# Two tanh to a step, and who copies the turned exponentials, in the interleaved attentions of an audio tower

## The reference, cut to what matters

```python
# third: one head, every query with every key through 16 tanh units
hid = tanh(hq[:, :, None, :] + hk[:, None, :, :] + b1)
attn = softmax(Q @ K.T / sqrt(128) + hid @ W2 + b2);  out = attn @ V
# fourth: 8 heads, causal
dot = where(causal, (x @ Wq.T / s) @ (x @ Wk.T / s).T, -inf)   # s = 128 ** 0.25
out = (softmax(dot) @ (x @ Wv.T)) @ Wo.T, summed over heads
```

## Time and profile before

| | us |
|---|---|
| median of 3 runs | 4598.27 (4597.84 to 4599.58) |
| the profiled execution, its own time | 4594.98 |
| its span, first to last instruction | 4593.1 |
| mean granted TensorE clock | 0.946 |
| busy, share of the span | PE 91%, DVE 61%, ACT 63%, POOL 15% |
| `tail()`, from about 3040 to the end | about 1550 |
| three passes of last with additive attention, each | about 240 |
| of each, the stretch that has tanh in it | 150 to 153 |
| last attention alone (sequence 3) | about 144 |

### The profile page before, as it was taken

One profiled execution on the slowest core, in us unless ns is written; L12 is line 12 of the kernel. 1 busy time (PEld: TensorE's weight loads), 2 busy tenths in 40 slices (PEclk: granted clock), 3 DMA queues, 4 the chain that ended last, 5 costly groups with the idle time before them and its releaser, 6 DMA issues.

```text
span 4593.1 us, 67780 instructions
## 1 busy us (share of the span) xinstructions
PE 4165.6 (91%) x25119; PEld 2334.1 (51%) x25119; DVE 2788.3 (61%) x6459; ACT 2872.6 (63%) x6125; POOL 692.7 (15%) x466
## 2 busy tenths in 40 slices
PE   6788779999999999999999999968888888997988
PEld 4454434444444444444444444434556655665666
DVE  5655567777777777777777777622343344245254
ACT  1222247877787877778777777765664474474533
POOL 0000112222222222222222222100000000000000
PEclk9877779999999999999999999979999999999999
DMA  2000034333342424242433424000100000100000
GB/s 108 1 28 0 21 45 53 46 46 55 41 69 37 57 43 53 50 53 44 52 50 53 57 36 59 24 31 24 36 1 19 26 1 10 31 1 1 28 4 4
DMA packets 94423, 160.53 MB, mean 35 GB/s; under 512 B 18272, under 2 KB 75024, under 8 KB 93712
## 3 DMA queue, kind: packets, MB, share of 16 engines
q1 hardware_dynamic: 94096, 156.20, 20.4%
HBM read 74.04 MB, written 7.82 MB: 18 GB/s over the span
## 4 chain that ended last, share of the span: by engine, by line
PE 74%; DVE 9%; issue 6%; ACT 6%; DVEq 2%; PEld 1%; POOL 1%; DMA 1%; PEldq 0%; POOLq 0%; SPq 0%; ACTq 0%
PE ps L1151 12%; PE ps L1187 12%; PE ps L1161 10%; PE ps L1507 9%; PE ps L1221 4%; PE ps L1230 4%; PE ps L1142 2%; PE ps L1038 2%; PE ps L1639 2%; PE ps L1250 2%; PE ps L1439 2%; DVE peaks L2225 2%; PE ps L1601 1%; PE ps L1577 1%; PE ps L1023 1%
## 5 line engine op out<-in xcount | busy, mean ns | idle before, releaser
L2225 DVE TENSOR_REDUCE peaks<-ps 128x1 f32<-128x748 f32 (+1 forms) x1536 | 1408.4, 933 | 481.8 <-PE ps L1161 459.6
L1796 ACT ACTIVATE masked<-ps 128x384 f32<-128x384 f32 (+3 forms) x1536 | 683.1, 486 | 197.2 <-PE ps L1151 185.0
L1796 ACT ACTIVATE probs<-ps 128x384 f32<-128x384 f32 (+1 forms) x1536 | 662.3, 484 | 74.1 <-PE ps L1151 73.6
L912 POOL TENSOR_TENSOR rstd<-var,minus_half 128x6 f32<-128x6 f32 x104 | 138.3, 1329 | 2875.2 <-DVE var L2458 1484.5
L1151 PE MATMUL ps<-shared 98*128 98x384 bf16 (+3 forms) x1536 | 447.3, 327 | 4.4 <-ACT probs L1796 1.7
L1151 PE MATMUL ps<-q_stack,k_stack 98*128 98x384 bf16 (+3 forms) x1536 | 449.9, 328 | 0.9
L1161 PE MATMUL ps<-k_stack,q_stack 96*128 96x374 bf16 (+1 forms) x1536 | 380.7, 329 | 37.0 <-DMA k_stack<-parts 21.5
L1161 PE MATMUL ps<-shared 96*128 96x374 bf16 (+1 forms) x1536 | 372.1, 323 | 8.7 <-DVE peaks L2225 8.0
L1151 PEld LDWEIGHTS ps<-shared 98*128 98x128 bf16 (+1 forms) x1536 | 147.9, 103 | 336.6 <-ACT masked L1796 125.9
L1151 PEld LDWEIGHTS ps<-q_stack,k_stack 98*128 98x128 bf16 (+1 forms) x1536 | 149.7, 103 | 328.4 <-ACT masked L1796 121.2
L1161 PEld LDWEIGHTS ps<-k_stack,q_stack 96*128 96x128 bf16 (+1 forms) x1536 | 154.6, 105 | 159.4 <-DVE peaks L2225 44.3
(11 more groups left out here) (571 smaller groups left out, 7684.6 us busy)
## 6 DMA issues: line engine op xcount, KB each, us to landing
shared<-parts SPq DMA_DIRECT2D x192, 187.0 KB, 9.2
wr<-in_l SPq DMA_DIRECT2D x32, 580.5 KB, 3.5
q_stack<-parts SPq DMA_DIRECT2D x96, 187.0 KB, 7.8
k_stack<-parts SPq DMA_DIRECT2D x96, 187.0 KB, 10.3
wts<-in_l SPq DMA_DIRECT2D x32, 514.5 KB, 3.6
wrow<-in_l_rows SPq DMA_DIRECT2D x32, 320.0 KB, 4.1
wq<-in_l SPq DMA_DIRECT2D x32, 192.0 KB, 3.3
const<-in_const SPq DMA_DIRECT2D x1, 4202.5 KB, 12.9
```

The lines of the kernel that those rows point to most:

```text
L912: pool.tensor_tensor(lane.rstd, lane.var, minus_half[:, :], ALU.pow).then_inc(S["rstd_ready"], 1)
L1796: act.activation(probs_ring(u)[0:m, 0:hi - lo], src[0:m, 0:hi - lo], ACT.Exp, scale=float(HD) ** -0.5).then_inc(S["ring_done"], 1)
L2225: v.tensor_reduce(peaks[0:m, g, j, head:head + 1], src[0:m, :, 0:T // 2], XY, ALU.max)\
```

## The change

Two edits. Each step `add` of four tanh (cost 3.95) becomes a step `add` (2.1) and a step `more` (1.85), two tanh each on ACT (the wait for a free buffer in the first, `hidden_ready` in the second, the exponentials of L1944 at the start of the second). The other engines do in `add` what they did and nothing in `more`. And ACT copies half 0 of the turned exponentials as well as half 1; DVE's L2591 goes.

```diff
-        steps += [(("add", u, q), 3.95) for u in range(NT) for q in range(4)]
+        steps += [step for u in range(NT) for q in range(4)
+                  for step in ((("add", u, q), 2.1), (("more", u, q), 1.85))]
...
-                def add(lane, k, u, q):
-                    if u == 0 and q == 0:
+                def add(lane, k, u, q, more=False):
+                    if u == 0 and q == 0 and not more:
                         act.drain()
                         used[0] = n.now("hidden_used")
+                        n.take(f"spread0_{k}", 2 * NT)
                         n.take("hidden_used", 4 * NT)
...
-                    if quad and s >= TANH_SLOTS:
+                    if quad and s >= TANH_SLOTS and not more:
                         act.wait_ge(S["hidden_used"], used[0] + s - TANH_SLOTS + 1)
-                    for i, (g, _) in enumerate(quad):
+                    first, end = (2, len(quad)) if more else (0, 2)
+                    for i, (g, _) in list(enumerate(quad))[first:end]:
                         if q == 1 and u and i == 2:
                             exponentials(lane, k)
...
-                    if quad:
+                    if quad and more:
                         last.then_inc(S["hidden_ready"], 1)
-                    elif q == 1:
+                    elif q == 1 and not quad:
                         exponentials(lane, k)
...
                 def last(lane, k, i):          # ACT
                     what, e, u = last_entry(i - SPREAD_LAG)
+                    if what == "score":
+                        tiles = min(3, u + 1)
+                        act.wait_ge(S[f"spread0_{k}"], n.take(f"spread0_{k}"))
+                        act.activation(flat(last_probsT(lane, i - SPREAD_LAG)[:, 0:tiles, :]),
+                                       ps[:, SPREAD_BANK, 0:tiles * P], ACT.Copy).then_inc(S[f"taken0_{k}"], 1)
...
                 def last(lane, k, i):          # DVE
-                    what, e, u = last_entry(i - SPREAD_LAG)
-                    if what == "score":
-                        tiles = min(3, u + 1)
-                        v.wait_ge(S[f"spread0_{k}"], n.take(f"spread0_{k}"))
-                        v.tensor_copy(flat(last_probsT(lane, i - SPREAD_LAG)[:, 0:tiles, :]),
-                                      ps[:, SPREAD_BANK, 0:tiles * P]).then_inc(S[f"taken0_{k}"], 1)
```

More of the change, by code:

```diff
@@ L1945, in exponentials @@
                                    accum_out=lane.total[:, 0:1]).then_inc(S[f"probs_ready_{k}"], 1)
-                def add(lane, k, u, q):
-                    if u == 0 and q == 0:
+                def add(lane, k, u, q, more=False):
+                    if u == 0 and q == 0 and not more:
                         act.drain()
                         used[0] = n.now("hidden_used")
+                        n.take(f"spread0_{k}", 2 * NT)
                         n.take("hidden_used", 4 * NT)
-                    if q == 0 and u < 2:
+                    if q == 0 and u < 2 and not more:
                         act.wait_ge(S["query_part_ready"], n.take("query_part_ready"))
                     quad, s = ADDITIVE[u][q] if u < NT else (), 4 * u + q
-                    if quad and s >= TANH_SLOTS:
+                    if quad and s >= TANH_SLOTS and not more:
                         act.wait_ge(S["hidden_used"], used[0] + s - TANH_SLOTS + 1)
-                    for i, (g, _) in enumerate(quad):
+                    first, end = (2, len(quad)) if more else (0, 2)
+                    for i, (g, _) in list(enumerate(quad))[first:end]:
                         if q == 1 and u and i == 2:
@@ L2036, in tail @@
                         mixed(lane, k, *at)
-                    elif what == "add":
-                        add(lane, k, *at)
+                    elif what in ("add", "more"):
+                        add(lane, k, *at, what == "more")
                     elif what == "pool":
@@ L2613, in last @@
                         v.drain()
+                        n.take(f"spread0_{k}", len(LAST_UNIT))
                 def logits(lane, k):
```

## The result

The changed kernel takes 4702.23 us (median of 4 runs, 4701.43 to 4708.41) against 4598.06 of the kernel before in the same rounds: a ratio of 1.0229, 95% interval 1.0211 to 1.0247. It is 104 us slower. The forecast was 4650 (+52) and the range ended at 4686: sign and place were right, the size was about half, and the time lies outside the range.

What follows compares the result with a forecast made beforehand. PE was taken to carry the time, with each in-order handover between ACT and PE adding to it. 3 x (19 - 4) + 9 = +54 us gave 4652, written as 4650 (chance 0.62), range 4608 to 4686.

Steps and rivals of the forecast that it cites:

- Last attention alone, +9: Last attention of sequence 3: half 0 copies queued on ACT cost 1.1 us a head, 8 heads; bounds 5 and 12.
- The 0.83 at u = 5: Last attention alone: ACT's copy stands behind the exponential of u = 4, so PE goes on 0.83 us late.
- u = 4: Last attention alone: ACT copies the queries first, so PE turns half 1 of this entry 0.25 us late.
- the small entries: Last attention alone: covered by 0.5 us or more of other PE work; up to 0.5 each where uncovered.
- End of a pass, -4: After the last tanh: DVE sheds copies, PE no longer waits for them behind pooling and gating; -1 to -6 us.
- Tanh stretch, +19: Per pass: PE waits for ACT's late copies and tanh; +16.9 us in 116 walked, some 2 elsewhere; bounds 8 and 26.
- the walk: Tanh stretch, L29 to L37 stepped through in the new order with old durations: five PE waits, +6.7 us; three neighbours likewise.
- the sparser rest, 36 us, adds some 2: The 36 us of a tanh stretch outside the four heads from L13 to L45: some 2 us more a pass.
- The finer steps pay: Rival: halved tanh blocks halve PE's idle time in the tanh stretch, -8 a pass; total -30, 4568 us; chance 0.10.
- Only the copy counts: Rival: tanh stretch only +6 a pass, end -4, last attention alone +9; total +15, 4613 us; chance 0.15.
- The clock falls too: Third rival: five more half-rate spells a pass after PE waits, 3 x 8.5 = +25 on top, 4677 us; chance 0.13.
- The upper bound: Tanh stretch: 26 us a pass, the worst segment's rate throughout, 6.7 / 26.2 of 152, less a third for the sparse end.

Runs made afterwards that it cites:

- the kernel with the wide copies only: Kernel before, steps of four tanh kept, with ACT copying half 0 only for entries u = 5, 3, 4: 4660.97 us, ratio 1.0134.
- the mildest form: Kernel before with only ACT's tanh split into steps of two; PE and DVE keep their old order, DVE its copy: 4604.17 us, ratio 1.0011.
- the fillers: Against the kernel with ACT copying half 0 for u = 5, 3, 4: 8 unused matmuls before PE's u = 5 wait, last attention alone: 4655.83 us.

## Why the prediction was right in direction and short in size

- **Where the kernel is bound: right.** PE carried the time, ACT had 36 us to spare and has 58 now; the kernel still lost, because what counts is when ACT reaches a copy. The five waits for copies and four for L1944 were read from PEld, the weight loads; the matmuls themselves waited three times for each, 5.3 and 3.5 us.
- **Last attention alone, +9: right in size** (+11.5), in part by luck. The seven later heads take 1.16 us more each (18.00 for 16.84) against 1.1 predicted; the first takes the other 3.4, with a half-rate spell in it.
- **How that +11.5 came about is only in part as walked.** The 0.83 at u = 5 came out in the kernel with the wide copies only. In a later head of the changed kernel PE's half 1 of u = 5 is 0.33 late: its wait is 0.75 for 0.61, and a new one of 0.48 for the copy of u = 2 stands where PE waited 0.51 for its next score slot before. u = 4 adds 0.27, as predicted (0.25), and the copy of u = 1, ahead of its weigh, some 0.5. The prediction had the small entries down as covered and took nothing for them into the sum. Five other kernels that leave this stretch as it was have 144.8 there, not 143.4, with 3.5 to 4.5 us more at half rate at its start, so one trace doesn't fix the length within a microsecond.
- **End of a pass, -4: right size (-3.5), wrong reason.** Fewer waits give 0.8; the rest is work that moved out and clock, and the ends are as short with the steps alone. The copy on ACT only there (-10 us, of which the ends show 6) confirms the direction, not the size.
- **Tanh stretch, +19: the step that failed**, in two terms. First, the walk itself held: five waits within 0.4 us each, four heads 18.8 for 16.9. But "the sparser rest, 36 us, adds some 2" was put down without a walk, and it measured 5.5: the first and the sixth head have 2.1 and 3.8 us more idle time, like the others. Rest and walk together are 5 of the 16 us that were missed. Second, the walk's durations were all those at full rate, and the clock stood beside the sum as a rival with 0.13. It measured 18 us more at half rate a pass, 9 us of lost work; the third rival (five more spells, +8.5 a pass) was right in mechanism and in the number of spells. Together 19 + 5 + 9 = 33, and 2 us are matmuls from the end.
- **The rivals.** "The finer steps pay" is refuted three times: with the old copies (+43, and +5 even in the mildest form), with ACT's copies (+104, and +108 with PE's old order, against +96), and with none of the tanh stretch's copies on ACT (+31). "Only the copy counts" is near the truth in its name and wrong in its size: the copy alone is +96 of the 104, not +15. "The clock falls too" happened, on top of the forecast: 4677 by its own sum; of the 25 us from there to the measured time the 5 us a pass of idle time above are the most.
- **The upper bound** of 26 for the tanh stretch was made from the worst segment's rate with no clock in it, so the range couldn't hold the case that the prediction itself called a rival.

Both terms are measured as sums of PE's idle and busy time, and a spell's price on the path could differ from the busy time it adds. The three passes run the same list of steps, so they can be compared. L13 to L21 before took 27.6, 26.0 and 27.6 us, with a spell, none and a spell in it; L21 to L29 after took 37.2, 35.5 and 35.5, with two spells, one and one. The idle time was the same in each, 3.3 and 6.0 us. So there a spell costs 1.6 us and makes no idle time. Over a whole stretch the price is less: after, the first pass has 20.5 us at half rate and takes 185.9, the others 27.3 and 187.8, that is 1.9 us for two spells. By these two rates the 18 us more at half rate cost 5 to 9 us a pass; how the 35 us divide between clock and waits is open by that much.

## What to carry to other kernels

Before moving a copy out of PSUM to the engine with more time to spare, look at what stands ahead of it in that engine's list at the moment it is needed: 0.07 us of a faster copy bought waits of up to 4.2. Cutting the work ahead of it into smaller steps hardly shortened those waits (32.0 to 30.3 us in the first tanh stretch); giving the copy to the other engine did. Where PE is the bound and a walk gives it many new waits, put the clock into the sum, not among the rivals: in this kernel each such spell was 3.4 us at half rate and cost 1 to 1.6 us on the path. And walk all heads, also the ones that look sparse or covered.

## What the runs showed of the hardware that was not expected

In the last attention alone with only the wide copies on ACT, one wait a head grew from 0.61 to 1.44 us, and right behind it every second head had a spell of 3.4 us at 0.50 (three of them, gone with the fillers). With all copies on ACT the lateness is spread over two waits a head (3.9 us in 8 for the small entries and 8.0 in 10 for the wide, by the waits of after), and there is one such spell in the whole stretch: the kernel that moves only some of the copies is 8 us slower there than the one that moves all. The heads show that this difference is the clock's: without a spell in it a later head takes 18.00 us in both kernels, with one 19.6. The waits themselves, one of 1.44 or one of 0.48 and one of 0.75, come to the same length.
